# The state product of a chunked delta-rule scan as two 64x128 tiles of the array instead of one 128x128 product

## What is computed

```
def step(S, inp):
    q_t, k_t, v_t, g_t, b_t = inp
    S = S * jnp.exp(g_t)[..., None, None]
    u = (v_t - jnp.einsum('bhk,bhkv->bhv', k_t, S)) * b_t[..., None]
    S = S + jnp.einsum('bhk,bhv->bhkv', k_t, u)
    o_t = jnp.einsum('bhk,bhkv->bhv', q_t, S)
    return (S, o_t)
```

## Time and profile before

| | us |
|---|---|
| median of 3 runs | 2637.5 |
| lowest, highest | 2637.27, 2646.81 |
| span of the profiled execution | 2632.2 |
| PE busy in it | 2266.7 (86%) |
| PE weight loads | 1651.1 (63%) |
| DVE busy | 1903.0 (72%) |
| ACT busy | 1354.1 (51%) |
| POOL busy | 1137.5 (43%) |

### The profile page before, as it was taken

One profiled execution on the slowest core, in us unless ns is written; L12 is line 12 of the kernel. 1 busy time (PEld: TensorE's weight loads), 2 busy tenths in 40 slices (PEclk: granted clock), 3 DMA queues, 4 the chain that ended last, 5 costly groups with the idle time before them and its releaser, 6 DMA issues. The chain is left out here.

```text
span 2632.2 us, 93819 instructions
## 1 busy us (share of the span) xinstructions
PE 2266.7 (86%) x36541; PEld 1651.1 (63%) x36542; DVE 1903.0 (72%) x3913; ACT 1354.1 (51%) x3667; POOL 1137.5 (43%) x1143
## 2 busy tenths in 40 slices
PE   4652999999987889899888989989898888989987
PEld 4541999999963646556565655746556565655646
DVE  5664232323228888988889899888988989888894
ACT  0001444344326655656656566655656656566663
POOL 3774444444433426253342624436253342624333
PEclk9997999999988999999999999999999999999998
DMA  5574222222210010100101000010100101000010
GB/s 168 193 248 152 72 72 73 71 72 72 72 55 21 17 44 11 36 22 25 32 15 44 21 27 23 25 44 5 42 22 25 33 14 44 23 24 22 25 29 16
DMA packets 105644, 135.05 MB, mean 51 GB/s; under 512 B 39360, under 2 KB 78816, under 8 KB 105056
## 3 DMA queue, kind: packets, MB, share of 16 engines
q0 software_dynamic: 23552, 61.38, 7.5%
q1 hardware_dynamic: 62448, 40.55, 5.8%
q10 hardware_dynamic: 19312, 28.33, 3.0%
HBM read 76.18 MB, written 54.00 MB: 49 GB/s over the span
## 5 line engine op out<-in xcount | busy, mean ns | idle before, releaser
L1458 DVE SCALAR_TENSOR_TENSOR att_cv<-att_psA,att_cw,att_cv 128x508 f32<-128x508 f32 (+2 forms) x660 | 479.2, 737 | 7.6
L1789 POOL TENSOR_TENSOR att_Sd<-att_S,att_mst 128x1024 f32<-128x1024 f32 x128 | 242.9, 1903 | 505.1 <-DVE att_S L1572 482.0
L999 PE MATMUL att_psA<-att_xt,att_wqkv 128*128 128x512 f32 x880 | 425.3, 616 | 17.0 <-DMA att_xt<-xn_cols 12.6
L1122 PE MATMUL att_psS<-att_W,att_ktok 128*128 128x128 f32 x2048 | 258.8, 280 | 12.1 <-DVE att_S L1572 6.4
L999 PEld LDWEIGHTS att_psA<-att_xt,att_wqkv 128*128 128x128 f32 x880 | 156.7, 193 | 178.7 <-issue 159.5
L734 PE MATMUL moe_psHT<-moe_xT,moe_w1s 128*128 128x128 f32 x2176 | 267.5, 276 | 0.0
L1122 PEld LDWEIGHTS att_psS<-att_W,att_ktok 128*128 128x128 f32 x2048 | 242.5, 193 | 32.9 <-issue 17.2
L675 ACT ACTIVATE moe_hT<-moe_psHT,moe_b1T 128x128 f32<-128x128 f32 x544 | 155.1, 368 | 201.1 <-PE moe_psHT L734 201.1
L744 PE MATMUL moe_psY<-moe_w,moe_hT 128*128 x1088 | 257.2, 379 | 0.0
L734 PEld LDWEIGHTS moe_psHT<-moe_xT,moe_w1s 128*128 128x128 f32 x2176 | 256.1, 193 | 0.2
L701 DVE TENSOR_TENSOR moe_y<-moe_psY,moe_b2b 128x256 f32<-128x256 f32 x136 | 57.8, 425 | 271.1 <-PE moe_psY L744 271.1
(11 more groups left out here) (247 smaller groups left out, 4382.1 us busy)
## 6 DMA issues: line engine op xcount, KB each, us to landing
expert_out<-moe_y POOLq DMA_DIRECT2D x136, 128.0 KB, 2.0
route_x_in<-in_L_attn_x_dram SPq DMA_DIRECT2D x64, 128.0 KB
xn_rows<-route_xn ACTq DMA_DIRECT2D x16, 512.0 KB, 3.6
xn_cols<-route_xnT ACTq DMA_DIRECT2D x16, 512.0 KB, 3.8
moe_w<-in_L_ffn_W_dram ACTq DMA_DIRECT2D x2, 4096.0 KB, 24.5
att_xt<-xn_cols SPq DMA_DIRECT2D x16, 512.0 KB, 4.4
att_xr<-in_L_attn_x_dram SPq DMA_DIRECT2D x64, 128.0 KB, 2.7
out_dram<-att_xr SPq DMA_DIRECT2D x256, 32.0 KB, 1.7
```

Of the source, the lines that this page charges most:

```text
L999: last = MM(pair_bank(m, j)[:, h, :], wqkv[:, c, (2 * j + h) * P:(2 * j + h + 1) * P], xt[:, c, :], start=(c == 0), stop=(c == DC - 1))
L1122: last = MM(pS[:, h // 4, 2 * DV * (h % 4):2 * DV * (h % 4) + 2 * DV], ktok[:, c % 2, h, :], W[:, h, 2 * two:2 * two + 2, :], start=True, ...
L1458: last = V.scalar_tensor_tensor(out=late, in0=by_lane(pair_bank(m, j)[:, h, :])[:, :, 0:LT - d], scalar=cw[:, 2 * j + h, TAPS - 1 - d:TAPS ...
L1789: G.tensor_tensor(new, old, bc(mst[:, par, c, 4 + 2 * two:6 + 2 * two, :], 3, DV), op=ALU.mult).then_inc(s["sd_done" if two else "sd_half" ...
```

## The change

W gets two slots instead of four: `W[partition, head, 2, v]`. Lane l goes to slot l % 2. So W is block-diagonal inside partitions 0 to 63 (lanes 0 and 1), and again inside partitions 64 to 127 (lanes 2 and 3). The state product then uses 64 partitions at a time: a matmul at tile position (0, 0) takes lanes 0 and 1, one at (64, 0) takes lanes 2 and 3. Each has 64 rows and 128 columns of the array, and they write to different banks of pS (bank b for pair b). A half is now four heads of all four lanes, not eight heads of two lanes.

`spread` writes a half with two ACT instructions over all 128 partitions, 4 heads x 64 elements each, multiplied by a 0/1 mask `in_pair` per partition, which zeroes the rows of the other slot; W needs no initial zeroes. DVE's and POOL's halves follow: S and Sd are cut by heads. The mask is made at the start by POOL (one memset for zeroes, four for ones), and ACT waits for these constants once.

```diff
-        R = sb("R", [P, HV]); W = sb("W", [P, H, LANES, DV])
+        R = sb("R", [P, HV]); W = sb("W", [P, H, 2, DV]); in_pair = sb("in_pair", [P, 2])
...
-                for h in range(H):
-                    last = MM(pS[:, h // 4, 2 * DV * (h % 4):2 * DV * (h % 4) + 2 * DV], ktok[:, c % 2, h, :], W[:, h, 2 * two:2 * two + 2, :],
-                              start=True, stop=True)
+                for h in range(4 * two, 4 * two + 4):
+                    for b in range(2):
+                        r = slice(DV * b, DV * b + DV)
+                        last = MM(pS[:, b, :].rearrange("p (l h v) -> p l h v", l=2, h=4)[:, :, h % 4, :], ktok[r, c % 2, h, :], W[r, h, :, :],
+                                  start=True, stop=True, tile_position=(DV * b, 0))
...
-                        last = MM(pC[r, 0, DV * h:DV * h + DV], AT[r, par, c * H + h, :], W[r, h, l, :],
+                        last = MM(pC[r, 0, DV * h:DV * h + DV], AT[r, par, c * H + h, :], W[r, h, l % 2, :],
...
+            act.wait_ge(consts, NCONST)
...
-                    for l in (2 * two, 2 * two + 1):
-                        r = lane_rows(l)
-                        last = A(W[r, :, l, :], heads(pC[r, 0, :]), ACT.Copy)
+                    hs = slice(4 * two, 4 * two + 4)
+                    for k in range(2):
+                        last = A(W[:, hs, k, :], heads(pC[:, 0, :])[:, hs, :], ACT.Copy, scale=in_pair[:, k:k + 1])
...
-                new, old = (t[:, 2 * two:2 * two + 2, :].rearrange("p l (h v) -> p h l v", h=H) for t in (S, Sd))
-                V.tensor_tensor(new, pS[:, :, :].rearrange("p b (h l v) -> p (b h) l v", l=2, v=DV), old,
+                new, old = (t[:, :, HV // 2 * two:HV // 2 * two + HV // 2] for t in (S, Sd))
+                V.tensor_tensor(new, pS[:, :, :].rearrange("p b (l x) -> p (b l) x", l=2), old,
...
-            G.memset(W[:, 0:4, :, :], 0.0).then_inc(consts, 1)
-            G.memset(W[:, 4:8, :, :], 0.0).then_inc(consts, 1)
-            G.wait_ge(consts, 8)
+            G.memset(in_pair[:, :], 0.0).then_inc(consts, 1)
+            G.wait_ge(consts, 7)
...
+            for l in range(LANES):
+                G.memset(in_pair[lane_rows(l), l % 2:l % 2 + 1], 1.0).then_inc(consts, 1)
...
-                new, old = (t[:, 2 * two:2 * two + 2, :].rearrange("p l (h v) -> p l h v", h=H) for t in (Sd, S))
-                G.tensor_tensor(new, old, bc(mst[:, par, c, 4 + 2 * two:6 + 2 * two, :], 3, DV),
+                hs = slice(4 * two, 4 * two + 4)
+                new, old = (t[:, :, :].rearrange("p l (h v) -> p l h v", h=H)[:, :, hs, :] for t in (Sd, S))
+                G.tensor_tensor(new, old, bc(mst[:, par, c, 4:4 + LANES, hs], 3, DV),
```

More of the change, by code:

```diff
@@ L814, in attention @@
         masks = ctx.enter_context(nc.semaphore("att_masks"))
-        NCONST = 10
+        NCONST = 9 + LANES
         ALONE = 20
@@ L1730, in _ @@
                             pattern=[[-1, P]], channel_multiplier=1).then_inc(consts, 1)
+            G.wait_ge(consts, 9)
+            for l in range(LANES):
+                G.memset(in_pair[lane_rows(l), l % 2:l % 2 + 1], 1.0).then_inc(consts, 1)
             G.wait_ge(consts, NCONST)
```

## The result

The changed kernel is faster. Its runs took 2569.4, 2574.5 and 2582.7 us against a median of 2639.5 us (2637.3 to 2646.8) for the kernel before. The ratio is 0.9745, with a 95% interval of 0.9712 to 0.9779. The profiled execution has a span of 2567.6 us, against 2632.2 before. The forecast was a span of 2569 and a time of 2574 us. A fourth execution of the changed kernel took 3641.6 us at a granted clock of 0.603, where these three have 0.972 to 0.974 and the four later ones 0.969 to 0.973; it is in no comparison here, and its cause is open.

The account below looks back on a forecast made before the run. PE was taken to set the scan, with DVE 1.65 us per chunk behind, and DVE the rest. Savings of 56 us in 15 groups plus 7 in the last, 63, took 2637.5 to 2574.5, say 2574; range 2553 to 2603.

Parts of the forecast that it names:

- What bounded the kernel, and that only DVE's waits come out: Scan: PE is full, DVE only 1.65 us per chunk behind, so a chunk falls only by what DVE waits.
- The product: State product on PE: each half's 16 passes overlap in two row tiles, 1.2 us against 1.98 and 1.82.
- The two switches: Changes of tile shape on PE around each half of the state product: 0.08 to 0.10 us each, 0.2 together.
- The spread: ACT's writing of W: four instructions take 1.56 us, not 2.40; t2 comes earlier, saving a third of its 6.9 us wait.
- The waits of DVE: Scan, 14 groups: product's 46.3 us all go, key read's 31.5 falls to 26.5, t2's 6.9 by a third.
- The last group: Attention's final group, without filler work: both products lie on the path, 1.4 to 1.8 us a chunk, 7 us for four.
- the clock: PE's granted clock could drop if PE idles more; counted in the range, not as a case, with 5 us allowed.
- The stretch with the inversion: After each group's scan: moves as a whole and keeps its length, since DVE sets it.
- After the change a middle chunk is DVE's: Middle chunk of the scan: 12.5 us, set by DVE, with PE at 11.9.
- the 2.0 us of that rival: No overlap: the tiles take turns in loads or array, 2.0 us per half of the product; 2642 us, chance 0.08.
- part overlap: Rival for the product on PE: about 1.6 us per half, PE stays the bound; 2594 us, chance 0.09.
- The loss that was priced at 193 ns a pass: Slower rival: each product pass pays its weight load in full, 3.3 us a half; 2804 us, chance 0.05.

Follow-up runs that it names:

- after_again: The changed kernel unedited, run again later as a reference beside later experiments: median 2578.3 us, 0.9779 of the kernel before.
- e10: The changed kernel with its fast product kept, but the spread cut into four ACT instructions of 64x256 per half instead of two of 128x256: 2685.8 us, ratio 1.0179.
- e5: The changed kernel with DVE's two expert-row instructions of each chunk on 16 instead of 256 columns: 2578.9 us.
- e1: The changed kernel with all eight passes of the upper tile ahead of the lower tile's eight: 2739.8 us, 0.9899; on the other chip 2617.4 us, 0.9906.

## Why the prediction was right, and where it was not

**What bounded the kernel, and that only DVE's waits come out: right.** The scan of the shown group gave back 4.1 us, against 4 x (0.89 + 0.73) = 6.5 us that PE has less to do on the product. From the first solve of the attention to that of the last group the time fell from 1697.0 to 1642.4 us, by 54.6; the forecast was 56 for 15 groups. DVE's waits fell by 50.3 us in 14 groups, so 54 in 15, which is the same number. The repeat, after_again, has 1648.0 us, so 49.0 us less than before: the size is good to some 6 us.

**The product: 1.2 us forecast, 1.09 measured.** The mechanism was right, and the loads overlap as the small tiles' loads had suggested. The term was 0.1 us too high, and the part of it that was mis-sized is the overlap: it was taken as 88%, 1.03 us for the passes, from tiles of 32x32. The pairs start within 0.007 us of each other, so eight of them 0.112 us apart are 0.89 us. The two switches were sized rightly at 0.2 us: the first distance and the one behind the last pair are 0.21 us each, 0.10 more than 0.112. It mattered little, since DVE came later than the product in either case.

**The spread: 1.56 us forecast, 1.57 measured.** In the shown chunk t's wait fell by 0.1 us (0.28 to 0.19), as forecast; over 14 groups 4.7 of its 6.9 us went, and not 2.3. What the text did not say is how near to the path the spread lies. "In the middle chunks this is hidden on PE's side" holds at 1.57 us and no longer at 3.37 (e10, 107 us). Lengths between these were not tried.

**The waits of DVE: right, one by one.** Product 46.3 to 5.7 (forecast 0), key read 31.5 to 26.5 (forecast 26.5), t 6.9 to 2.2. The middle chunk is 12.39 us where 12.5 was forecast, PE's work in it 12.39 - 0.59 = 11.8 where it was 11.9.

**The last group: 10 us, forecast 7.** It fell from 65.5 to 55.5 us (56.0 in the repeat). From solve to solve its chunks took 14.49, 13.53 and 15.53 us before and 10.15, 12.07 and 12.54 after, so 4.3, 1.5 and 3.0 us less, and from the last solve to the end it is 1.3 us less. Only the second chunk shows the forecast's 1.4 to 1.8 us by itself. The first and third hold some 4 us of the clock as well, which leaves 6 us for the change. Before, the first solve of that group took 1.93 us and the product behind it 3.78, which is TensorE's lower level (1.2 GHz, the same rows take 1.10 and 2.05 at 2.4); PE had waited 1.58 us for DVE ahead of them. After, it had waited 0.67 us, and they took 1.10 and 1.16, at the upper level. At the third solve it is the same: 1.93 us for the solve and 1.11 for the transposes behind it before, 1.10 and 0.66 after; there PE had waited 1.63 us ahead in both kernels, so the wait alone does not tell them apart. The first rows before, then after:

```profile
2566.68 1.93 PE L1105 MATMUL att_psC<-att_R,att_Y 32*32 32x64 f32 x64 [1.58 <-DVE att_Y L1546]
2569.91 3.78 PE L1122 MATMUL att_psS<-att_W,att_ktok 128*128 128x128 f32 x16 [1.29 <-ACT att_W L1352]
```
```profile
2512.13 1.10 PE L1105 MATMUL att_psC<-att_R,att_Y 32*32 32x64 f32 x64 [0.67 <-DVE att_Y L1549]
2514.18 1.16 PE L1124 MATMUL att_psS<-att_W,att_ktok 64*128 64x128 f32 x16 [0.95 <-ACT att_W L1355]
```

Over the 53 us from about that solve the granted clock was 0.87 before (2567 to 2620) and 0.94 after (2512 to 2565). I had counted the clock as a risk only. That the sum came within 2 us of the profiled span is in part luck: the groups and the last group's own part fell short by 1 to 2 us each, and these 4 us, put at nothing, made it up.

**The stretch with the inversion: forecast 0, and right within the scatter.** Between PE's marks it is 0.6 us longer in the shown group and 5.7 us in 15 groups (941.2 to 946.9). But DVE sets it, and between marks of DVE (its last state add, L1572 or L1575, and the next group's L1494 or L1497) it went from 61.72 to 61.58 us in the shown group; in 15 groups from 957.1 to 960.0, and 956.1 in the repeat. PE waits longer for ACT's keys before L1042, 15.9 us in 14 groups against 9.0. That wait lies ahead of PE's mark, so in the scan.

**"After the change a middle chunk is DVE's": too simple.** DVE is busy all of the chunk but 0.63 and 0.19 us, as was said, yet e5 took 0.45 us of its work away in each chunk and gained nothing clear of the scatter. The sum did not rest on it.

**The rivals.** No kernel here has the two tiles and no overlap at all. In turns they take 1.64 us, since three pairs still overlap; the 1.98 us estimated without them fit the 2.0 us of that rival, and its 2642 us stay untried. By its number e1 is nearly what the prediction called part overlap (1.6 us, 2594 us forecast), but it measured 2617, 23 us more, so that rival's time was too low. The loss that was priced at 193 ns a pass does not exist; loads come every 61 ns.

## What to carry to other kernels

Where two matmuls each fill half the rows of the array, issue them alternately, tile by tile, and look at the time from start to start in the trace: in turns the same passes took 1.64 us, alternately 1.09. Before you count on it, see what the engine that waits for the product does instead; here DVE's waits, and not PE's freed time, gave the 15 groups to within 2 us in one trace and 7 in the repeat. And a relief that follows such a change should be tried against all engines, since shorter DVE work, an earlier key read and a spread in two instructions each gave nothing clear of the scatter, while a longer spread cost 107 us.

## What the runs showed of the hardware

- Two 64x128 tiles run side by side: 16 passes of 128 columns in 1.09 us, with their weight loads covering 61 ns each, against 1.82 us and 118 ns for the full array. A pass of either kind starts every 112 ns; with the tiles alternating two start at once (7 ns apart). With eight passes of one tile ahead of eight of the other only three pairs do, and it is 1.64 us.
- A change of tile shape costs 0.10 us here: the first start-to-start distance of the product and the one behind its last pair are 0.21 us in place of 0.11.
- The lock between DVE and POOL can be placed by a few tenths of a microsecond of timing: R at 736 ns when it begins at the decay's end, 900 ns on average when it begins 0.4 us earlier; a 12-column add at 0.16 or 0.95 us; an expert row at 0.48 or 1.38. POOL's power of 8 elements (L1812, 1.64 to 1.97 us) ran beside such instructions of DVE without holding them (in the changed kernel the expert row at 1552.29 took 0.48 us, 1551.03 to 1553.00 being L1812's).
